# A two-layer gated cross-attention kernel: biases folded into the last row of the weights, bias products removed, and new instruction orders

## What is computed

```python
x = x + tanh(g_xattn[0]) * L0_xattn(layernorm(x), ctx)   # 4 heads; q, k, v, o products; bias bo after o
x = x + tanh(g_ffn[0])   * L0_ffn(layernorm(x))          # x @ (W + low-rank).T + b
x = x + tanh(g_xattn[1]) * L1_xattn(layernorm(x), ctx)   # 1 head; biases bq, bk, bv
x = x + tanh(g_ffn[1])   * L1_ffn(layernorm(x))          # 16-head self-attention (b_qkv) + 8 experts, top 2
                                                         # (b_gate, b_experts)
```

## Time and profile before

| what | value |
|---|---|
| median of 3 runs | 900.35 us (899.77 to 902.41) |
| the profiled execution's own time | 901.12 us |
| its span, first to last instruction | 899.3 us |
| mean granted TensorE clock | 0.981 of full speed |
| busy share of the span: PE, DVE, ACT, POOL | 94%, 76%, 62%, 43% |
| instructions on PE, DVE, ACT, POOL | 11828, 1657, 1240, 731 |

### The profile page before, as it was taken

The page is one execution under the profiler, slowest core; times in us unless marked ns, Lnnn a source line. Parts: engine busy times, 40 slices in busy tenths (PEclk is TensorE's granted clock), DMA queues, the critical chain, the costliest instruction groups (busy, mean ns, idle before and its releaser), DMA issues. The chain is left out here.

```text
span 899.3 us, 34510 instructions
## 1 busy us (share of the span) xinstructions
PE 849.3 (94%) x11828; PEld 678.3 (75%) x11828; DVE 685.0 (76%) x1657; ACT 556.3 (62%) x1240; POOL 384.4 (43%) x731
## 2 busy tenths in 40 slices
PE   4688999999999999999999999999999999999886
PEld 2467877878878777888777888878777888777664
DVE  2678888778877877887788778877877887787653
ACT  2654766666666666666666666666666666666443
POOL 5213345444334445433445444334545433444435
PEclk9779999999999999999999999999999999999998
DMA  9112222122122212222222122122212212221100
GB/s 315 54 51 65 74 80 71 53 66 76 55 68 77 77 51 60 77 59 62 77 77 66 54 67 73 53 73 77 76 48 63 77 58 64 77 60 57 39 7 12
DMA packets 40543, 61.78 MB, mean 69 GB/s; under 512 B 5248, under 2 KB 27030, under 8 KB 40378
## 3 DMA queue, kind: packets, MB, share of 16 engines
q1 hardware_dynamic: 40508, 61.32, 23.2%
HBM read 48.41 MB, written 12.89 MB: 68 GB/s over the span
## 5 line engine op out<-in xcount | busy, mean ns | idle before, releaser
L1251 POOL TENSOR_SCALAR ln_ve<-ln_mv 112x1 f32<-112x1 f32 x128 | 30.9, 242 | 370.5 <-DVE ln_mv L991 370.4
L1329 POOL TENSOR_TENSOR part<-part 112x256 f32<-112x256 f32 x224 | 163.0, 733 | 13.6 <-POOL part L1329 4.1
L835 ACT ACTIVATE part<-bankE,cgS 112x256 f32<-112x256 f32 x256 | 107.1, 472 | 9.3 <-issue 1.7
L333 PE MATMUL bankE<-wexs_hi,xT_hi 128*112 128x512 f16 x256 | 98.9, 387 | 6.7 <-ACT part L835 3.5
L333 PE MATMUL bankE<-wexs_lo,xT_hi 128*112 128x512 f16 x256 | 97.0, 379 | 0.0
L333 PE MATMUL bankE<-wexs_hi,xT_lo 128*112 128x512 f16 x256 | 97.0, 379 | 0.0
L1255 POOL TENSOR_TENSOR ln_rs<-ln_ve,cst 112x1 f32<-112x1 f32 x128 | 72.7, 568 | 10.7
L1012 DVE TENSOR_REDUCE mx<-quad 112x2 f32<-112x750 f32 x64 | 57.2, 934 | 22.3 <-PE quad L429 22.3
L1091 DVE TENSOR_TENSOR p_lo<-p2T,p_hi 112x896 f16<-112x896 f32 x64 | 67.2, 1090 | 6.2 <-ACT p_hi L820 6.1
L1133 DVE TENSOR_REDUCE mx<-quad 112x8 f32<-112x896 f32 x64 | 66.2, 1075 | 1.7 <-PE quad L565 1.7
L812 ACT ACTIVATE p2T<-quad 112x896 f32<-112x896 f32 x64 | 58.5, 919 | 10.2 <-PE quad L585 10.2
(11 more groups left out here) (236 smaller groups left out, 3259.4 us busy)
## 6 DMA issues: line engine op xcount, KB each, us to landing
ctf<-in_ctx_T SPq DMA_DIRECT2D x32, 375.0 KB, 4.3
ctn<-in_ctx_n SPq DMA_DIRECT2D x32, 375.0 KB
hold<-kvA SPq DMA_DIRECT2D x32, 281.2 KB, 2.6
kc<-hold SPq DMA_DIRECT2D x32, 187.5 KB
xin<-in_x SPq DMA_DIRECT2D x32, 112.0 KB, 2.5
x<-in_x SPq DMA_DIRECT2D x32, 112.0 KB, 2.1
out_x<-xout SPq DMA_DIRECT2D x32, 112.0 KB, 1.9
wex<-in_w_exp SPq DMA_DIRECT2D x1, 2048.0 KB, 11.0
```

The costliest lines, as they stand in the source:

```text
L333: last = mm(o, w, m, start=(n == 0), stop=(n == len(terms) - 1))
L835: act.activation(part[:, e, :], bankE[0:LQ, n * D:(n + 1) * D], ACT.Identity, scale=cgS[:, e:e + 1])\
L1329: pool.tensor_tensor(part[:, k, :], part[:, k, :], part[:, k - 1, :] if k else x3[:], ALU.add).then_inc(moe_sum[j].sem, 1)
```

## The change

**The ones column.** For the layer norms 1, 2 and 3 column 255 of the normalised tile `xn` is set to 1.0 once, at the start, and `normalise` now writes 255 columns instead of 256. Since the 256 normalised values sum to zero, the last one is minus the sum of the others; the old last row of the weights is therefore subtracted from the 255 other rows, and the bias takes its place as the last row. The result is the same. Norm 0 stays as it was, and so does the bias product of `project_o`.

**Products.** The bias products of `ffn0`, `query_keys`, `project_vg`, `project_qk` and `experts` are gone, 12 per item. The one-time product that made the bias for `query_keys` (`l1b` with `l1k`) is gone as well.

**Setting up.** The packing of those biases is gone from DVE, ACT and POOL. POOL now subtracts the old last rows, once: `less_l1q` and `less_t2` and `less_wf`, `less_wqk`, `less_wvg` and four times `less_wex`. The rows to subtract arrive as a block repeated over all 128 partitions (`last`, 128 by 2824 float32 values, 1.4 MB), in three transfers. The weights' high and low parts wait for the subtraction.

**Orders.** The bodies of PE, ACT, DVE, POOL and SP are all written in a new order, rotated as well: on PE an iteration now begins with `scores0_T`, which was its middle, so that the second half of the old iteration i is the first half of the new iteration i+1. There are 37 iterations as before.

The diff, cut to its core:

```diff
         t1 = sb("t1", [RANK, D])
-        t2 = sb("t2", [UDIM, D])
+        t2, t2d = sb("t2", [UDIM, D]), sb("t2d", [UDIM, D])
...
+        NR = D + NQK + NVG + E * D
+        last = sb("last", [P, NR])
...
             def load_weights(a):
                 if first(a):
-                    for t, w in ((wqk, w_qk), (wvg, w_vg), (bex_f, b_exp), (stack_f[:, DN:NST - 2 * D], b_stack)):
-                        sp.dma_start(t[:], w).then_inc(ffn1_in, DMA)
+                    for t, w in ((wqk[:], w_qk), (wvg[:], w_vg), (last[:, D:NR - E * D], last_rows[:, D:NR - E * D])):
+                        sp.dma_start(t, w).then_inc(ffn1_in, DMA)
                     sp.dma_start(wex[:], w_exp).then_inc(experts_in, DMA)
+                    sp.dma_start(last[:, NR - E * D:NR], last_rows[:, NR - E * D:NR]).then_inc(experts_in, DMA)
@@ SP body @@
                 if A and not first(a): load_x(a)
-                if FF: store(f)
+                if A: load_weights(a)
+                if A and more: load_ctx_T(a + 1)
+                if C: load_ctx_n(c)
+                if A: hold_context(a)
                 if B: load_x0(b)
-                if C: load_ctx_n(c)
-                if A and more: load_ctx_T(a + 1)
-                if B: fetch_held(b)
-                if A: hold_context(a)
-                if A: load_weights(a)
+                if C: fetch_held(c)
+                if EE: store(e)
@@ PE @@
-                    pe.wait_ge(lora_s.sem, lora_s.after("t2", 0))
+                    pe.wait_ge(l1q_s.sem, l1q_s.after("less_last", 0))
...
-                    group(bankE[0:2, 0:DN], [(l1b[:, c, :], l1k[:, c, :]) for c in range(KD)]).then_inc(A_s.sem, 1)
...
-                    h[:, c, :], l[:, c, :], lin_hi[:, WF, c, :], lin_lo[:, WF, c, :])] + [(ones16, b_f)]).then_inc(f0_s.sem, 1)
+                    h[:, c, :], l[:, c, :], lin_hi[:, WF, c, :], lin_lo[:, WF, c, :])]).then_inc(f0_s.sem, 1)
...
-                        A_hi[:, c, cols], A_lo[:, c, cols], h[:, c, :], l[:, c, :])] + [(b_A[:, cols], ones16)])
+                        A_hi[:, c, cols], A_lo[:, c, cols], h[:, c, :], l[:, c, :])])
...
-                        wqk_hi[:, c, cols], wqk_lo[:, c, cols], h[:, c, :], l[:, c, :])] + [(b_qk[:, cols], ones16)])
+                        wqk_hi[:, c, cols], wqk_lo[:, c, cols], h[:, c, :], l[:, c, :])])
...
-                    h[:, c, :], l[:, c, :], wvg_hi[:, c, :], wvg_lo[:, c, :])] + [(ones16, b_vg)]).then_inc(vg_s.sem, 1)
+                    h[:, c, :], l[:, c, :], wvg_hi[:, c, :], wvg_lo[:, c, :])]).then_inc(vg_s.sem, 1)
...
-                    wex_lo[:, c, cols].rearrange("p e n -> p (e n)"))]
-                    + [(ones16, bex[:, 2 * j * D:2 * (j + 1) * D])]).then_inc(moe[j].sem, 1)
+                    wex_lo[:, c, cols].rearrange("p e n -> p (e n)"))]).then_inc(moe[j].sem, 1)
...
@@ PE body @@
+                if C: scores0_T(0, c)
+                if C: scores0_T(1, c)
+                if FF: values2(f)
+                if B: project_k(b)
+                if EE: norm_T(3, e, bankD, pv2, "norm", e - 1)
+                if B: project_v(b)
+                if DD: norm_T(2, d, bankC, f0_s, "x2", d)
+                if C: values0(c)
+                if EE: project_vg(e)
+                if B: lora_3(b)
+                if DD: query_keys(d)
                 if C: out0_T(c)
+                if EE: project_qk(e)
                 if DD: scores1(d)
+                if C: project_o(c)
+                if DD: max1_T(d)
                 if EE: experts(0, e)
                 if DD: scores1_T(d)
                 if EE: scores2(e, b, c)
                 if B: norm_T(0, b, bankB, wo_s, "x1", b - 1)
                 if DD: sums1(d)
+                if A: lora_1(a)
                 if EE: experts(1, e)
                 if EE: max2_T(e)
+                if B: project_q(b)
+                if EE: scores2_T(e)
+                if A: lora_2(a)
                 if DD: out1(d)
                 if EE: experts(2, e)
                 if B: scores0(b)
                 if C: norm_T(1, c, bankC, o1_s, "x3", c - 1)
                 if EE: experts(3, e)
                 if B: max0_T(b)
                 if C: ffn0(c)
+                if A: layer1_A(a)
@@ ACT body @@
...
+                if A: lora_t1(a)
+                if A: wv_hi(a)
...
+                if DD: exp1(d)
                 if EE: weigh_experts(0, e)
+                if B: xT_hi(0, b, bankB, qs, "ps")
                 if DD: sums1_copy(d)
                 if EE: max2_copy(e)
+                if A: wqo_hi(a)
...
+                if A: lora_t2(a)
...
                 if A: ctxT_hi(a)
...
@@ DVE @@
-                ts(xn[n][:], src[:], ln_mv[n][:, 0:1], ln_rs[n][:], ALU.subtract, ALU.mult).then_inc(ln[n].sem, 1)
+                w = D if n == 0 else D - 1
+                ts(xn[n][:, 0:w], src[:, 0:w], ln_mv[n][:, 0:1], ln_rs[n][:], ALU.subtract, ALU.mult).then_inc(ln[n].sem, 1)
...
@@ DVE body @@
+                if B: lora_add(b)
+                if EE: xT_lo(3, e, bankD, moe[NG - 1], "ps")
+                if B: keys_lo(b)
+                if B: normalise(0, xin, b)
...
                 if DD: max1(d)
                 if A: wv_lo(a)
                 if B: values_lo(b)
                 if C: residual(wo_s, "x1", c, x1, bankB, x0, f0_s, "x2", 1)
+                if EE: gate_max(e)
+                if DD: wqk_lo_half(d)
+                if EE: gate_index(e)
+                if EE: gate_indexf(e)
                 if EE: q2_lower(e)
+                if EE: gate_recip(e)
                 if C: stats(1, x1, wo_s, "x1", c)
                 if EE: max2(0, e)
+                if EE: k2_lower(e)
                 if EE: max2(1, e)
+                if B: xT_lo(0, b, bankB, qs, "ps")
...
@@ POOL @@
+            for n in range(1, 4):
+                pool.memset(xn[n][:, D - 1:D], 1.0).then_inc(filled, 1)
...
+            def less(ch, w0, w1, row):
+                pool.tensor_tensor(w0, w0, row, ALU.subtract)
+                pool.tensor_tensor(w1, w1, row[0:P - 1], ALU.subtract).then_inc(ch.sem, 1)
...
+            def less_wex(j, b):
+                if first(b):
+                    pool.wait_ge(experts_in, 2 * DMA)
+                    es = slice(2 * j, 2 * j + 2)
+                    less(wex_s[j], wex[:, 0, es], wex[0:P - 1, 1, es], last_ex[:, es])
...
@@ POOL body @@
+                if FF: finish(f)
+                if A: gate_wo(a)
+                if B: gate_wf(b)
+                if EE: gate_pick(e)
+                if C: less_wex(3, c)
+                if A: gate_b_o(a)
+                if EE: gate_combine(e)
+                if EE: gate_weights(e)
+                if C: less_wex(2, c)
+                if A: ctxT_hi(a)
+                if A: less_l1q(a)
+                if B: gate_wv(b)
+                if A: less_t2(a)
+                if B: less_wex(0, b)
                 if C: rstd(1, c)
+                if A: less_wf(a)
+                if EE: add_experts(0, e)
+                if C: gate_wvg(c)
                 if EE: add_experts(1, e)
                 if DD: rstd(3, d)
                 if C: rstd(2, c)
+                if B: less_wex(1, b)
                 if A: rstd(0, a)
+                if A: less_wvg(a)
+                if A: less_wqk(a)
                 if EE: add_experts(2, e)
                 if EE: add_experts(3, e)
```

More of the change, by code:

```diff
@@ L175, in flamingo_kernel @@
         gates_s = chain("gates_s", "tanh scaled")
-        gated_s = chain("gated_s", "wo b_lin wf wv wvg b_vg")
+        gated_s = chain("gated_s", "wo b_o wf wv wvg")
         blin_s = chain("blin_s", "scaled half packed")
[L179 to L188, removed]
+        lora_s = chain("lora_s", "ps1 t1 ps2 t2 less_last ps added")
+        l1q_s = chain("l1q_s", "less_last")
+        A_s = chain("A_s", "ps hi lo")
+        wk_s, wv_s, wqo_s = (chain(n + "_s", "hi lo") for n in ("wk", "wv0", "wqo"))
+        wf_s, wqk_s, wvg_s = (chain(n + "_s", "less_last hi lo") for n in ("wf", "wqk", "wvg"))
+        wex_s = [chain(f"wex{j}_s", "less_last hi lo") for j in range(NG)]
         ct_in, cn_in, x_in = chain("ct_in", "c", DMA), chain("cn_in", "c", DMA), chain("x_in", "x", DMA)
@@ L350, in lora_3 @@
                 if first(b):
-                    pe.wait_ge(lora_s.sem, lora_s.after("t2", 0))
+                    pe.wait_ge(lora_s.sem, lora_s.after("less_last", 0))
                     for c in range(KD):
-                        last = mm(bankD[:, c * D:(c + 1) * D], t2[:, c * P:(c + 1) * P], uaT[:], start=True, stop=True)
-                    last.then_inc(lora_s.sem, 1)
+                        end = mm(bankD[:, c * D:(c + 1) * D], t2d[:, c * P:(c + 1) * P], uaT[:], start=True, stop=True)
+                    end.then_inc(lora_s.sem, 1)
             def layer1_A(a):
@@ L847, in body @@
+                if C: wex_hi_copy(3, c)
                 if EE: weigh_experts(1, e)
[L848 to L857 removed]
@@ L1261, in gate_wo, with gate_b_o, less_wf, less_t2 @@
```

(37 more changed lines are left out.)

264 lines of the change are left out of this document (86 added, 178 removed).

## The result

The changed kernel takes 914.06 us (median of 4 runs, 911.05 to 918.06), the kernel before beside it 901.23 (899.77 to 902.41). The ratio is 1.0126, its 95% interval 1.0092 to 1.0159: the kernel became 1.3% slower where 865 us were forecast. The profiled execution is the slowest of the four (918.06 us); it spans 916.3 us.

A forecast was written before the change was run, and what follows sets the result against it. PE was taken as full (742.7 of 750 us). 901.1 - 39.4 (products) + 3 (hand-offs) + 3.4 (start) - 2 (products outside the 29 intervals) = 866.1, median 0.8 lower: 865 us; own range 857 to 873, 8 in 10 850 to 881.

The forecast's parts named there:

- Moved behind more work is `fetch_held`: SP's key fetch behind 1.47 MB of other transfers: lands at 447.3, wanted by `scores1` at 448.9; hidden, 1.1 us spare.
- keys fetched late: Rival: `scores1` waits for SP's late key fetch, each interval stalls 1.9 us, 920 us; chance 0.04.
- Its threshold: Late-keys rival: cost begins when keys land over 1.1 us late, a loss from 1.1 + 1.36 = 2.5 us on.
- both rings: Repeating waits: `ctxT_lo`, SP's queue, fetch, `scores1` and next scores; and gate weights `cgS`, `experts(1)`, next `project_vg`.
- The gate ring: Rival: `cgS` comes late for `weigh_experts(0)`, `experts(1)` waits, 0.5 us per interval, 880 us; chance 0.13.
- inside its slack: nothing: Gate weights `cgS` up to 1 us later on DVE and POOL, within 1.5 us of slack before ACT: no cost.
- The products: Bias products removed from PE, priced by distances between starts: 1.36 us per item, 39.4 us over 29 intervals.
- hand-offs 0.1 us: Lost cover at small waits between engines: 0.1 us per interval against the gain, +3 us over 29 intervals.
- The prediction's fear for `scores0` behind the exponential: On PE, `scores0` waits for ACT's second exponential; without `experts(2)`'s 0.21 us the wait grows by 0.21, nothing won.
- the new orders move cover to where it is wanted: On PE, `out1` behind `scores2_T` gives about 0.97 us more cover; `project_q` covers 0.7 us for `scores2_T`.
- The start: First `project_k` at 17.2 instead of 13.80, +3.4 us (0 to +13); rival with POOL's and SP's work exposed 875, chance 0.04.
- DVE: Sign of a right forecast: DVE's busy time per interval stays 20 to 21 us.

The follow-up runs named there:

- e3: Changed kernel with both e1's early key fetch and e2's early gate steps: 873.6 us, ratio 0.9661 to the kernel before.
- e1: Changed kernel with one SP call moved: `fetch_held` ahead of `load_ctx_T`, `load_ctx_n`, `hold_context` and `load_x0`; 878.2 us, ratio 0.9721 to the kernel before.
- e5: Kernel before, products and engine orders kept, with SP's body in the changed kernel's order (keys fetched late): 944.3 us, ratio 1.0461.
- e6: e3 with the 12 products put back, a tile of zeros in place of the bias: 903.8 us, ratio 1.0018 to the kernel before.
- e4: Kernel before with the folding alone (ones column, subtractions, no bias products), all engine bodies in the old orders: 897.9 us, ratio 0.9954.
- e10: e7 with the first `layer1_A` back behind `lora_3` on PE and ACT's first context copy early: 885.5 us, ratio 0.9807 to the kernel before.
- e7: e3 with ACT's `weigh_experts(2)` moved ahead of `probs2_hi(0)`: 886.0 us, ratio 0.9814 to the kernel before.
- e12: e7 with ACT's `ctxT_hi` also moved behind `max0_copy`, so the maxima are copied earlier: 875.7 us, ratio 0.9707 to the kernel before.
- e2: Changed kernel with DVE's `gate_max`, `gate_index` and `gate_indexf` moved earlier, the fetch still late: 906.5 us, ratio 1.0032 to the kernel before.
- e8: Changed kernel with two unused transfers of 32 bytes each ahead of the key fetch: 914.0 us, ratio 1.0147 to the kernel before.
- e9: Changed kernel with two unused transfers of 112 KB each ahead of the key fetch: 939.4 us, ratio 1.0438 to the kernel before.
- e11: Changed kernel with `fetch_held` directly behind `load_ctx_T`, still behind SP's wait for `ctxT_lo`: 885.3 us, ratio 0.9813 to the kernel before.

## Why the prediction was wrong

**The failed step is "Moved behind more work is `fetch_held`".** The prediction put the transfers at 4.7 us plus 2 for issue and landing, and ended at "it stays hidden, with about 1.1 us to spare". From the issue of `load_ctx_T` to the first product with the keys it took 408.51 - 398.87 = 9.6 us, 2.9 us more than the 6.7 reckoned (9.8 on average). The cover was reckoned well: 447.3 + 1.1 - 440.6 = 7.8 us, measured 407.3 - 398.9 = 8.4. The size of the transfer term was wrong, and its source: 315 GB/s is what the start's large weight transfers reach; in this stretch 123 to 208 GB/s were moved. The page of the kernel before had nearer rows, its DMA issues with KB each and us to landing, and the prediction didn't use them:

```profile
ctf<-in_ctx_T SPq DMA_DIRECT2D x32, 375.0 KB, 4.3
...
hold<-kvA SPq DMA_DIRECT2D x32, 281.2 KB, 2.6
```

These are 87 and 108 GB/s. By them 1.47 MB would have been bounded by 4.7 us from below and some 14 to 17 us from above, and 1.1 us of slack could not have been called safe. The rival "keys fetched late" had the mechanism right, with 0.04 where it deserved far more. Its reckoning of the wait fits: 2.9 us longer, less 0.6 us of additional cover and 1.1 us of slack, is the wait of 1.2 us of the iteration shown.

Its threshold does not. A loss was to begin at 2.5 us late, since 1.36 us of gain had to be used up first; with the cover counted the keys were 2.3 us late, and a wait of 1.3 us by itself would have left the time about where it was. The kernel became slower because the gain was smaller as well. In us per interval, from before: -0.98 for products and orders with both rings mended (e3), +0.22 for the gate (e1 to e3), +1.30 for the keys (e1 to after; good to 0.2), together +0.54.

**A wait on a transfer is repeated in each iteration.** The 1.3 us are not caught up; they are paid 29 times, as e1 and e5 show from both sides. The way round is read from the bodies, not measured link by link: when PE stands still, ACT and DVE fall behind with it, `ctxT_lo` comes later, and SP's queue starts later by the same amount. What is measured is its outcome: the distance from SP's issue to the moment at which PE is ready for the keys stays at 8.45 us however long PE waited the iteration before.

**The gate ring** was called nothing, with 0 to 0.5 us per interval as ends; it is 0.22 to 0.23. It was a named rival (0.13) and came true at half its size beside the other. The step that failed is "inside its slack: nothing". The slack of 1.5 us became a wait of 0.84.

**The products** were priced at 1.36 us by distances between starts. Put back into the mended kernel they cost 0.99 (e3 to e6). With both rings mended the interval is 24.93 against the forecast 24.65. If the products keep their price, the term "hand-offs 0.1 us" was 0.38, inside its ends of -0.5 and 0.5. The Trainium skill's figures (TensorE: Matmul & The Clock Gate, Back-to-back issue gap) gave 1.2 us; that lies nearer to the measured value, but by luck: in e3 products of 512 columns still start 0.21 to 0.22 us apart (412.12, 412.33, 412.55, 412.76), not 0.13. The rest may be lost cover or price; no run separates the two.

**Cover.** The prediction's fear for `scores0` behind the exponential is borne out by e4: the wait there grows by 0.2 us per iteration, and the old orders keep 0.48 of 1.36 us. So is its reading that the new orders move cover to where it is wanted: that wait is back at its old length in e3, and the interval gains 0.50 us.

**The start.** `project_k` was put at 17.2 and comes at 19.88, since `layer1_A` waits for POOL's first subtraction:

```profile
16.33 3.75 PE L329 MATMUL bankC<-l1k,l1q 128*128 128x256 f32 x8 [2.58 <-POOL l1q L1233]
19.88 0.83 PE L329 MATMUL quad<-kvA,linw_hi 128*128 128x375 f16 x2
```

Yet item 1 is only 1.55 us late, under the +3.4 forecast, and e10 gains nothing there. The sum was near, partly by luck. POOL's subtractions, counted as 13 in one place and 17 in another, are 17 and take 19.9 us in all, where 19.6 were reckoned. The 12.1 us by which e4's item 1 is late show that the fill can lose much with these additions; in the new orders it doesn't.

**DVE** was put at 20 to 21 us per interval and is 534.06 / 660 x 26.45 = 21.4, a little more, and still 5 us below the interval.

## What to carry to other kernels

A transfer moved down an in-order queue has to be priced with the bytes now ahead of it, at the rate that the same transfers reach in the same stage, not at the best rate of the profile; when the slack left is smaller than what that rate is uncertain by, the late arrival is the likely case. Removing work from the full engine also removes cover: the gain comes only where other work takes its place, and here it took new orders to turn 0.48 us into 0.98. In these fourteen kernels a loop that is paced by its engines repeats to 0.02 us, and one that waits for a transfer does not (below); this can be seen before any wait is looked up.

## What the runs showed of the hardware that was not expected

**The transfer rate in the loop.** 208, 187 and 123 GB/s were moved with the DMA engines busy for 67%, 68% and 44%. The packets go at 275 to 310 GB/s for the 16 engines while they are busy (each rate by its share), and a third of the engines' time stays empty while SP issues the nine transfers, more when the last of them run out. The Trainium skill (DMA: Bandwidth & Descriptors, Bandwidth) gives 341 GB/s for one transfer of 1 MB from HBM to SBUF that GpSimd issues; the trace does not reach that for 1.5 MB in nine transfers to and from HBM. What leaves the engines empty was not tried.

**Steady and unsteady intervals.** In e1 the distances between successive `p1T` copies are 25.12 us from item 3 to item 28, each time. In the changed kernel they go from 25.9 to 29.7 there. All eight kernels in which no engine is listed as waiting for a transfer between 120 and 780 us (before, e1, e3, e4, e6, e7, e10, e12) repeat to 0.02 us; the six with such a wait (after, e2, e5, e8, e9, e11) scatter by 0.7 us (e11) to 3.8 us. The run times show less of it: the kernel before ranges from 899.8 to 906.9 us over all its runs, the changed one from 911.1 to 918.1.

The steady distances are 25.98 us before, 25.52 in e4, 25.88 in e6 and 24.89 in e3. By these the new orders alone win 0.10 us, and products and orders together 1.09; the interval from items 1 and 30 takes in the ends of the loop, where the new orders give that back.

**A POOL instruction of one column can take six times as long.** The variance step of the layer norm (variance plus a small constant), in the page's groups and in POOL's timeline of the changed kernel, and DVE's beside it:

```profile
L1199 POOL TENSOR_SCALAR ln_ve<-ln_mv 112x1 f32<-112x1 f32 x128 | 81.8, 639 | 214.4 <-DVE ln_mv L944 214.4
```

```profile
423.66 1.36 POOL L1199 TENSOR_SCALAR ln_ve<-ln_mv 112x1 f32<-112x1 f32 x1 [3.80 <-DVE ln_mv L944]
```

```profile
423.42 1.06 DVE L1045 TENSOR_TENSOR p_lo<-p2T,p_hi 112x896 f16<-112x896 f32 x1
```

The mean was 242 ns before and is 639 now; the shortest takes 0.21 us. In the new order it falls beside DVE's subtractions with two operands from SBUF: of the 128 in the changed kernel, 30 start while the subtraction shown runs and take 1.33 us on average, 27 start during the same step of the first layer and take 0.84, and those that start while DVE is idle or at its reciprocal take 0.21 to 0.23. By the Trainium skill (GPSIMD Engine Reference, Specifications) GpSimd contends with such DVE instructions; the trace agrees. It adds 51 us of POOL's busy time in all. No listed wait of PE names it, and e3, the fastest kernel here, has the same mean of 639; what it costs was not tried.
